# VectorE's low half of the next expert's second weights, moved behind the output operations in a mixture-of-experts loop

## Chip, cores and metric

One NeuronCore of a Trainium2 chip runs the program. The metric is the device time of one execution in microseconds, the median of several runs.

## The reference

The whole computation is one block of a graph network on 1250 nodes with 768 features: a layer norm, then a graph convolution over 20000 edges and a second-order linear attention over 12 heads, both added to the input, then a second layer norm and a switch layer of eight experts. Only the expert part is touched here:

```python
h = jax.nn.gelu(jnp.einsum('ecd,edf->ecf', buf[:E], w1) + b1[:, None, :], approximate=False)
o = jnp.einsum('ecf,efd->ecd', h, w2) + b2[:, None, :]
y_exp = o[routes, dest_c]
y = jnp.where(keep[:, None], y_exp, xf)
out = y * prob_max[:, None]
```

Each of the 8 experts has room for 195 rows (capacity), `w1` is 768 x 384 and `w2` 384 x 768 per expert. The result of each row, weighted by its gate, is added to the row before the switch layer.

## The kernel before

Everything runs in float32 accuracy, made of two reduced numbers: a matrix `A` is split into a high half `AH` (a rounded copy, made by ScalarE) and a low half `AL = A - AH` (made by VectorE), and each product is the three matmuls high x high, high x low and low x high (`product`, lines 2022 to 2030).

The expert loop is software-pipelined by hand over five engines, each with its own program and semaphores between them. Two experts are one turn of the `Fori` loop (`b` = 0, 1); the last pair is unrolled. For expert `e`:

- SyncE loads the weights into one staging buffer each, `w1s` and `w2s` (1152 KB each), and the second bias `b2r`. Its queue is in order: the bias of `e + 1` when the additions of `e - 1` are done (line 1776), the first weights of `e + 2` when VectorE has made `w1L` of `e + 1` (line 1780), the second weights of `e + 2` when it has made `w2L` of `e + 1` (line 1783).
- GpSimd issues the indirect transfers: it gathers the rows of `e + 2` (`xe`, line 1810), scatters the finished rows of `e` in two tiles of 105 and 90 rows (`out`, line 1839), and behind each scatter gathers the residual rows of `e + 1` (`x1g`, line 1818). When both scatters of `e` have landed (line 1845) it raises `oe_store` (line 1846), which lets VectorE write `oE` again.
- TensorE does the first product in three parts (line 2002), turns the rows of `e + 1` (line 1985), then does the second product in two tiles (line 2011). The second part of the first product waits until VectorE has read the second product of the expert before out of PSUM (`y_done`, line 2001).
- ScalarE makes `w1H` of `e + 1` (line 1857), the GELU and its high half `hH` (lines 1884, 1887), the high half of the turned rows (line 1869), and `w2H` of `e + 1` (line 1861).
- VectorE makes, in this order: `w1L` of `e + 1` (line 1903), the three parts of `hL` (line 1948), a small copy of the bias (line 1921), the three parts of `xeL` of `e + 1` (line 1927), a small copy of the gates (line 1932), `w2L` of `e + 1` (line 1907), and then for each of the two tiles an addition of the bias out of PSUM (line 1960, waits for the tile and for `oe_store`) and a scaling with the residual added (line 1965, waits for `x1g`). The four operations of lines 1960 and 1965 are the output operations.

`w2L` of `e + 1` is read by TensorE's second product of `e + 1`, one turn later, which waits for it at line 2008.

Of the kernel before, what the change touches and what calls it, by code (L numbers as in the profile page):

```python
# [89 lines left out]
def at(start, size):  # L90
    return bass.ds(start, size)
# [12 lines left out]
def build(nc, x, src, dst, gnn_w, gnn_b, w_qkv, b_qkv, w_proj, b_proj, sw, sb_, w1, b1, w2, b2, out,  # L104
          counts, keyd, vdram, odram, xfd, x1d, invd, lowd):
    ctx = ExitStack()
    with ctx:
# [14 lines left out]
        def right(stack, specs):  # L122
# [104 lines left out]
            ("PM", [T, N], F32), ("Ba", [T, NT, T], BF16), ("Bb", [T, N], BF16), ("same", [T, T], F32),  # L227
            ("place_i", [T, CAP], I32), ("place", [T, CAP], F32), ("far", [1, 2, E], F32)])
        _, csum, seatr, low, peak, heavy, mark, hid = region([
            ("before", [P, 4 * D + 6 * D], F32), ("csum", [T, 2, T], F32), ("seatr", [T, NT, HEAVY], F32R),  # L230
            ("low", [HEAVY, 2 * T], F32R), ("peak", [T, NT, NT], F32), ("heavy", [T, NT], F32),
# [71 lines left out]
        @block.sync  # L303
        def _(sp):
            for i in range(NT):
                move(sp, xn[:, i, :], x[i * T:(i + 1) * T, :], x_in[i // 2])
                if i == 1:
                    for wc in range(3):
                        sp.dma_start(w_staging(wc), w_parts[0][0][2 * wc * P:2 * (wc + 1) * P, :].rearrange(
                            "(k p) n -> p k n", p=P)).then_inc(w_early[wc], 16)  # L310
            sp.wait_ge(keys, 2)
            sp.dma_start(keyd[0:P, :], keyA[:]).then_inc(key_out, 16)
            sp.dma_start(keyd[P:, :], keyB[:]).then_inc(key_out, 16)
            for s_ in (1, 0):
                sp.dma_start(ws[:, s_], w_qkv[:, s_ * D:s_ * D + P].rearrange("(k p) n -> p k n", p=P)
                             ).then_inc(wqk_in[s_], 16)
            sp.wait_ge(key_out, 32)

            def load_keys(half, slot, c, n):

                sp.dma_start(kb[:, half, slot:slot + n, :], keyd[c:c + n, :].unsqueeze(0).broadcast_to([P, n, P])
                             ).then_inc(kb_in[half], 16)

            load_keys(0, 0, 0, EC)
            sp.wait_ge(w_lo, 3)
            load_keys(1, 0, EC, EC)
            for i in range(NT):
                sp.wait_ge(v_lo, 2 * i + 2)
                move(sp, vdram[:, i, :].rearrange("(j p) f -> p j f", p=T),
                     VS[:, i % 2].bitcast(F32).rearrange("p (j a) l f -> p j (a l f)", a=2), v_store[i % 2])  # L330
                if i == FIRST_EDGES + 1:
                    sp.wait_ge(idx_ready, 2)
                    load_keys(0, 0, 2 * EC, EC)
                if i == FIRST_EDGES + 3:
                    sp.wait_ge(idx_ready, 4)
                    load_keys(1, 0, 3 * EC, EARLY - 3 * EC)
                    load_keys(1, EARLY - 3 * EC, LONE, 1)
# [226 lines left out]
        def _(pe):  # L564
            pe.wait_ge(consts, 2)

            def turn_x(g):

                t0, nt = XGROUPS[g]
                pe.wait_ge(xn_done, t0 + nt)  # L570
                for u in range(FIRST_UNIT[g], FIRST_UNIT[g + 1]):
                    _, _, k0, nk = XUNITS[u]
                    if u >= 4:
                        pe.wait_ge(xt_lo, u - 3)
                    for k in range(nk):
                        for t in range(nt):
                            m = (k * nt + t) * T
                            ins = pe.transpose(ps[:, u % 4, m:m + T], xn[:, t0 + t, (k0 + k) * P:(k0 + k + 1) * P],
                                               ident[0:T, 0:T])
                    ins.then_inc(tr_done, 1)  # L580
# [1152 lines left out]
        def nodes_over(eng):  # L1733

            eng.wait_ge(agg_mm, NT)
            eng.wait_ge(pj_mm, NT)
            eng.wait_ge(lg_mm, NT)
            eng.wait_ge(ch_done, NT)
            eng.wait_ge(xf_done, NT)
            eng.wait_ge(lg_done, NT)  # L1740
            eng.wait_ge(x1_store[0], MOVED * NT // 2)
            eng.wait_ge(x1_store[1], MOVED * NT // 2)
# [153 lines left out]
        @block.vector  # L1896
        def _(dve):
            nodes_over(dve)
            order = Chain(dve, route_order, steps_before[0])

            def split_w1(e, b):
                dve.wait_ge(we_hi, 2 * e + 1)
                dve.tensor_tensor(w1L[:, b], w1s[:], w1H[:, b].bitcast(F32), ALU.subtract).then_inc(we_lo, 1)

            def split_w2(e, b):
                dve.wait_ge(we_hi, 2 * e + 2)
                dve.tensor_tensor(w2L[:, b], w2s[:], w2H[:, b].bitcast(F32), ALU.subtract).then_inc(we_lo, 1)

            split_w1(0, 0)
            dve.memset(x1g[:], 0.0)  # L1910
            dve.wait_ge(plain_store[0], MOVED * NT // 2)
            dve.wait_ge(plain_store[1], MOVED * NT // 2)
            dve.memset(xeH[:, :, CAP:].bitcast(F32), 0.0)
            dve.memset(xeL[:, :, CAP:].bitcast(F32), 0.0).then_inc(pads, 1)
            split_w2(0, 0)
            dve.wait_ge(b1_tr, 1)
            dve.tensor_copy(b1c[:].rearrange("p e m -> p (e m)"), ps[:, 3, 256:256 + E * FT]).then_inc(b1_done, 1)
            dve.wait_ge(b1_done, 1)

            def bias_of(e, b):  # L1920
                dve.tensor_scalar(b1cur[:, b, :], b1c[:, at(e, 1), :].rearrange("p o m -> p (o m)"), 1.0, None,
                                  ALU.mult).then_inc(b1cur_done, 1)

            def cut_rows(e):
                for n in range(3):
                    dve.wait_ge(xe_hi, 3 * e + (n + 1))
                    dve.tensor_tensor(xeL[:, 2 * n:2 * n + 2, 0:CAP],
                                      ps[:, n, 0:2 * CAPP].rearrange("p (k c) -> p k c", k=2)[:, :, 0:CAP],
                                      xeH[:, 2 * n:2 * n + 2, 0:CAP].bitcast(F32), ALU.subtract).then_inc(xe_lo, 1)

            def chance_of(e, b):
                dve.tensor_scalar(pcur[:, b, :], pmc[:, at(e, 1), :].rearrange("p o t -> p (o t)"), 1.0, None,
                                  ALU.mult)

            dve.sem_inc(y_done, FREE)
            dve.sem_inc(oe_done, FREE)
            bias_of(0, 0)
            chance_of(0, 0)
            cut_rows(0)

            def turn(m, last):
                for b in range(2):
                    e = 2 * m + b
                    if not (last and b == 1):
                        split_w1(e + 1, 1 - b)
                    for f in range(FT):
                        dve.wait_ge(hh_done, 3 * e + (f + 1))
                        dve.tensor_tensor(hL[:, f, :], h32[:, f, :], hH[:, f, :].bitcast(F32),
                                          ALU.subtract).then_inc(hl_done, 1)
                    if not (last and b == 1):  # L1950
                        bias_of(e + 1, 1 - b)
                        cut_rows(e + 1)
                        dve.wait_ge(oe_done, 2 * e + FREE)
                        chance_of(e + 1, 1 - b)
                        split_w2(e + 1, 1 - b)
                    dve.wait_ge(b2_in[b], m * 16 + 16)
                    for t, (r0, n) in enumerate(CTILES):
                        dve.wait_ge(m2_mm, 2 * e + (t + 1))
                        dve.wait_ge(oe_store, e + FREE)
                        dve.tensor_tensor(oE[0:n, t, :].rearrange("p (c d) -> p c d", c=2),  # L1960
                                          ps[0:n, 6 - 2 * t:8 - 2 * t, 0:HALF],
                                          b2r[0:n, b, :].rearrange("p (c d) -> p c d", c=2), ALU.add).then_inc(y_done, 1)
                        dve.wait_ge(y_done, 2 * e + (t + 1 + FREE))
                        dve.wait_ge(x1g_in[t], 16 * e + 16)
                        dve.scalar_tensor_tensor(out=oE[0:n, t, :], in0=oE[0:n, t, :], scalar=pcur[0:n, b, t:t + 1],
                                                 in1=x1g[0:n, t, :], op0=ALU.mult, op1=ALU.add).then_inc(oe_done, 1)

            with dve.Fori(0, LASTM) as m:
                turn(m, False)
            turn(LASTM, True)  # L1970
# [89 lines left out]
```

## Time and profile before

| what | value |
| --- | --- |
| median of three runs | 1019.64 us (1017.2 to 1021.0) |
| the profiled execution | 1020.73 us, of which the span of the core's instructions 1019.0 us |
| granted TensorE clock, mean | 0.948 of full speed |
| busy over the span | TensorE 89%, VectorE 75%, ScalarE 48%, GpSimd 35% |
| expert loop | from about 882 us to the end, some 135 us |
| chain that ended last, whole span | TensorE 55%, VectorE 18%, issue 11%, DMA 7% |

The busy shares are means over stages with different limits; the expert loop is the last eighth of the span. In the timelines below a row gives the start, the duration, the engine, the line of the kernel, the operation, what it writes and reads with shapes, how many such are merged in the row, and in brackets how long the engine was idle before it and what ended that.

### The profile page before, as it was taken

How to read it: one execution, taken by the hardware profiler on the slowest of the kernel's cores; microseconds unless marked ns; L12 is line 12 of the kernel's file. 1: busy time of each engine (PE TensorE's matmuls, PEld its weight loads, DVE VectorE, ACT ScalarE, POOL GpSimd, SP SyncE). 2: the span in 40 equal slices, each digit the busy share in tenths (PEclk: the TensorE clock that was granted, in tenths of full speed). 3: DMA queues.
4: the chain of work that ended last, by engine and by line, in shares of the span. 5: the costliest groups of instructions: out<-in, count | busy, mean ns of one | idle time of the engine just before them, and what ended most of it. 6: DMA issues, size and time to landing. Idle time of an engine off the chain costs nothing.

```text
span 1019.0 us, 15414 instructions
## 1 busy us (share of the span) xinstructions
PE 906.3 (89%) x5154; PEld 859.9 (84%) x5154; DVE 760.4 (75%) x1570; ACT 488.4 (48%) x720; POOL 359.7 (35%) x236
## 2 busy tenths in 40 slices
PE   2899789989989989999999899979999995499895
PEld 2899689989989989988988789969999995398884
DVE  6778459989989989989988798554666666567773
ACT  2221256766766766767667641340323222255540
POOL 1014455545445554654555620000000001526562
PEclk9899799999999999999999899998999995599998
DMA  9986462364464364355436379255676634767861
GB/s 275 353 146 176 93 123 32 65 114 81 63 114 81 60 113 78 59 110 83 66 44 146 57 118 207 60 147 129 186 204 183 168 122 132 213 200 239 273 203 47
DMA packets 137614, 136.70 MB, mean 134 GB/s; under 512 B 70561, under 2 KB 118276, under 8 KB 136545
## 3 DMA queue, kind: packets, MB, share of 16 engines
q1 hardware_dynamic: 109646, 119.29, 44.9%
q0 software_dynamic: 27520, 16.67, 11.7%
q8 instruction: 25, 0.41, 0.2%
q10 hardware_dynamic: 403, 0.17, 0.1%
q14 instruction: 20, 0.16, 0.1%
HBM read 94.31 MB, written 38.17 MB: 130 GB/s over the span
## 4 chain that ended last, share of the span: by engine, by line
PE 55%; DVE 18%; issue 11%; DMA 7%; ACT 5%; POOL 1%; SPq 1%; DVEq 0%; ACTq 0%; POOLq 0%
PE ps L2027 9%; PE ps L2028 9%; PE ps L2029 9%; PE ps L1202 7%; PE ps L1186 4%; PE ps L1187 4%; PE ps L1623 3%; DMA out<-oE,ids 3%; DVE Pl L1061 3%; PE ps L1624 3%; DVE Ph L1059 2%; ACT Ph L852 2%; DMA Cs<-counts 2%; PE ps L1162 1%; ACT Pf L874 1%
## 5 line engine op out<-in xcount | busy, mean ns | idle before, releaser
L388 POOL DMA_INDIRECT counts<-countc,idxu x157 | 274.3, 1747 | 258.6 <-DMA counts<-countc,idxu 222.5
L1061 DVE SCALAR_TENSOR_TENSOR Pl<-Pf,Ph 125x832 fp32r<-125x832 f32 (+1 forms) x180 | 184.2, 1027 | 44.0 <-ACT Ph L852 40.4
L874 ACT ACTIVATE Pf<-ps 125x832 f32<-125x832 f32 (+1 forms) x180 | 156.0, 867 | 127.2 <-PE ps L1187 119.1
L1202 PE MATMUL ps<-Ph,vsb 125*128 125x416 f32 (+1 forms) x360 | 133.4, 371 | 23.2 <-DVE Pl L1061 23.0
L1202 PE MATMUL ps<-Pl,vsb 125*128 125x416 f32 (+1 forms) x360 | 127.9, 355 | 0.0
L1202 PEld LDWEIGHTS ps<-Ph,vsb 125*128 125x128 f32 x360 | 68.6, 191 | 39.1 <-DVE Pl L1061 26.0
L2027 PE MATMUL ps<-wH,XH 128*125 128x384 f32 x240 | 84.5, 352 | 4.1 <-DVE wL L481 4.1
L2027 PE MATMUL ps<-XH,wqkH 128*128 128x416 f32 (+1 forms) x216 | 83.1, 385 | 4.4 <-DVE wqkL L299 2.4
L2028 PE MATMUL ps<-wL,XH 128*125 128x384 f32 x240 | 82.9, 346 | 0.0
L2029 PE MATMUL ps<-wH,XL 128*125 128x384 f32 x240 | 82.6, 344 | 0.0
L852 ACT ACTIVATE Ph<-Pf 125x832 fp32r<-125x832 f32 (+1 forms) x90 | 80.5, 895 | 0.8
L2029 PE MATMUL ps<-XH,wqkL 128*128 128x416 f32 (+1 forms) x216 | 77.4, 358 | 0.0
L2028 PE MATMUL ps<-XL,wqkH 128*128 128x416 f32 (+1 forms) x216 | 77.1, 357 | 0.0
L1623 PE MATMUL ps<-HH,CH 125*125 125x384 f32 (+1 forms) x200 | 69.0, 345 | 2.7 <-issue 1.8
L1202 PEld LDWEIGHTS ps<-Pl,vsb 125*128 125x128 f32 x360 | 69.0, 192 | 0.8
L1624 PE MATMUL ps<-HL,CH 125*125 125x384 f32 x200 | 68.5, 342 | 0.0
L1186 PE MATMUL ps<-MA,KHA 128*125 128x416 f32 (+1 forms) x180 | 66.3, 369 | 1.8 <-DVE MA L938 1.8
L1186 PE MATMUL ps<-MB,KHB 128*125 128x416 f32 (+1 forms) x180 | 65.5, 364 | 0.2 <-ACT Pf L874 0.2
L1187 PE MATMUL ps<-MB,KLB 128*125 128x416 f32 (+1 forms) x180 | 64.1, 356 | 0.0
L1187 PE MATMUL ps<-MA,KLA 128*125 128x416 f32 (+1 forms) x180 | 63.9, 355 | 0.0
L1059 DVE TENSOR_SCALAR Ph<-Pf 125x832 fp32r<-125x832 f32 (+1 forms) x90 | 55.1, 612 | 4.9 <-PE ps L1202 1.1
L1805 POOL MEMSET xe<- 105x1536 f32 x1 | 1.4, 1382 | 159.2 <-DVE lg L1450 159.2
(281 smaller groups left out, 2196.2 us busy)
## 6 DMA issues: line engine op xcount, KB each, us to landing
Cs<-counts SPq DMA_DIRECT2D x17, 546.9 KB
w1s<-L_ffn_w SPq DMA_DIRECT2D x8, 1152.0 KB, 6.4
w2s<-L_ffn_w SPq DMA_DIRECT2D x8, 1152.0 KB
odram<-OHL SPq DMA_DIRECT2D x12, 625.0 KB, 8.4
oS<-odram SPq DMA_DIRECT2D x10, 750.0 KB, 4.8
vdram<-VS SPq DMA_DIRECT2D x10, 672.0 KB
vsb<-vdram SPq DMA_DIRECT2D x12, 560.0 KB
kt<-keyd SPq DMA_DIRECT2D x5, 1280.0 KB
```

The costliest lines, as they stand in the source:

```text
L388: pool.indirect_dma_start(out=counts, out_offset=bass.IndirectOffsetOnAxis(ap=idxu[:, c:c + 1], axis=0), in_=countc[:, c:c + 1], in_offset ...
L852: act.activation(Ph[:, i % RING, :, 0:w], Pf[:, i % RING, :, 0:w], ACT.Identity, bias=1.0).then_inc(p_hiA, 1)
L874: act.activation(Pf[:, i % RING, :, 0:w], ps[0:T, 2 * (i % 2):2 * (i % 2) + 2, 0:w], ACT.Square, bias=1.0).then_inc(sq_done, 1)
L1061: dve.scalar_tensor_tensor(out=p, in0=f, scalar=1.0, in1=h.bitcast(F32), op0=ALU.add, op1=ALU.subtract).then_inc(p_lo, 1)
L1186: pe.matmul(out_, KH[a][:, kt * T:(kt + 1) * T], q, start=True, stop=False)
L1187: ins = pe.matmul(out_, KL[a][:, kt * T:(kt + 1) * T], q, start=False, stop=True)
L1202: ins = pe.matmul(ps[:, 4 + s % 2, 0:w], vsb[:, 2 * kp + t, a, :], part[:, m % RING, t, 0:w], start=(kp == 0 and t == 0 and part is Ph), s ...
L1623: pe.matmul(ps[0:T, b, 0:HALF], CH[0:k, i % 2, s_, :], HH[0:k, s_, cs], start=(s_ == 0), stop=False)
L1624: ins = pe.matmul(ps[0:T, b, 0:HALF], CH[0:T, i % 2, s_, :], HL[:, s_, cs], start=False, stop=(s_ == NT - 1))
L2027: pe.matmul(out, lh, rh, start=(k == 0), stop=False)
L2028: pe.matmul(out, lh, rl, start=False, stop=False)
L2029: ins = pe.matmul(out, ll, rh, start=False, stop=(k == tiles - 1))
```

## The change

In VectorE's program, `w2L` of the next expert is made behind the four output operations of the turn and not in front of them. It is still not made in the last turn. No other engine's program is changed, and no wait is added or removed.

```diff
                         cut_rows(e + 1)
                         dve.wait_ge(oe_done, 2 * e + FREE)
                         chance_of(e + 1, 1 - b)
-                        split_w2(e + 1, 1 - b)
                     dve.wait_ge(b2_in[b], m * 16 + 16)
                     for t, (r0, n) in enumerate(CTILES):
                         dve.wait_ge(m2_mm, 2 * e + (t + 1))
...
                         dve.scalar_tensor_tensor(out=oE[0:n, t, :], in0=oE[0:n, t, :], scalar=pcur[0:n, b, t:t + 1],
                                                  in1=x1g[0:n, t, :], op0=ALU.mult, op1=ALU.add).then_inc(oe_done, 1)
+                    if not (last and b == 1):
+                        split_w2(e + 1, 1 - b)
```

## Rows read from the trace of the kernel before

**Rows 1.** The chain that ended last, one turn of the loop: start us, us, what holds it.

```profile
948.62 0.52 issue
...
952.07 0.66 POOL out L1839
...
957.94 6.04 DMA out<-oE,ids
```

**Rows 2.** Timeline of VectorE, turns 3 and 4: start us, us, engine line operation output<-inputs.

```profile
948.64 0.96 DVE L1960 TENSOR_TENSOR oE<-ps,b2r 105x768 f32<-105x768 f32 x1 [1.51 <-POOLq L1846]
...
951.65 1.01 DVE L1965 SCALAR_TENSOR_TENSOR oE<-oE,pcur,x1g 90x768 f32<-90x768 f32 x1
952.59 2.55 DVE L1903 TENSOR_TENSOR w1L<-w1s,w1H 128x2304 fp32r<-128x2304 f32 x1
955.06 0.62 DVE L1948 TENSOR_TENSOR hL<-h,hH 128x196 fp32r<-128x196 f32 x2
956.84 0.36 DVE L1948 TENSOR_TENSOR hL<-h,hH 128x196 fp32r<-128x196 f32 x1 [1.15 <-ACT hH L1887]
...
960.01 2.56 DVE L1907 TENSOR_TENSOR w2L<-w2s,w2H 128x2304 fp32r<-128x2304 f32 x1 [1.10 <-ACT w2H L1861]
964.16 0.96 DVE L1960 TENSOR_TENSOR oE<-ps,b2r 105x768 f32<-105x768 f32 x1 [1.59 <-POOLq L1846]
```

**Rows 3.** Timeline of VectorE at the first and second output operations.

```profile
899.08 2.56 DVE L1907 TENSOR_TENSOR w2L<-w2s,w2H 128x2304 fp32r<-128x2304 f32 x1 [1.21 <-ACT w2H L1861]
901.56 0.95 DVE L1960 TENSOR_TENSOR oE<-ps,b2r 105x768 f32<-105x768 f32 x1
...
917.51 0.96 DVE L1960 TENSOR_TENSOR oE<-ps,b2r 105x768 f32<-105x768 f32 x1 [1.95 <-POOLq L1846]
```

**Rows 4.** Timeline of VectorE: output operations of experts 5 and 6.

```profile
979.31 0.96 DVE L1960 TENSOR_TENSOR oE<-ps,b2r 105x768 f32<-105x768 f32 x1 [1.23 <-POOLq L1846]
...
993.15 0.95 DVE L1960 TENSOR_TENSOR oE<-ps,b2r 105x768 f32<-105x768 f32 x1
```

**Rows 5.** Timeline of GpSimd: its calls for indirect transfers, with their time.

```profile
876.01 2.41 POOL L1810 DMA_INDIRECT xe<-xfd,ids  x1 [0.30 <-issue]
...
904.59 1.01 POOL L1839 DMA_INDIRECT out<-oE,ids  x1 [16.59 <-DVE oE L1965]
905.91 3.34 POOL L1818 DMA_INDIRECT x1g<-x1d,ids  x1 [0.30 <-DVE oE L1965]
...
920.94 3.94 POOL L1839 DMA_INDIRECT out<-oE,ids  x1 [0.30 <-issue]
...
952.07 4.21 POOL L1839 DMA_INDIRECT out<-oE,ids  x1 [0.30 <-issue]
...
957.94 0.98 POOL L1839 DMA_INDIRECT out<-oE,ids  x1 [0.30 <-issue]
```

**Rows 6.** Timeline of VectorE beside three of these calls.

```profile
874.95 2.54 DVE L1907 TENSOR_TENSOR w2L<-w2s,w2H 128x2304 fp32r<-128x2304 f32 x1
...
904.56 1.02 DVE L1965 SCALAR_TENSOR_TENSOR oE<-oE,pcur,x1g 90x768 f32<-90x768 f32 x1
905.51 2.54 DVE L1903 TENSOR_TENSOR w1L<-w1s,w1H 128x2304 fp32r<-128x2304 f32 x1
```

**Rows 7.** Timeline of all engines: TensorE's last matmul of expert 0's first output tile.

```profile
899.46 0.33 PE L2029 MATMUL ps<-w2H,hL 128*105 128x384 f32 x1
```

**Rows 8.** Timeline of SyncE's queue: issue of expert 7's first weights.

```profile
970.91 0.38 SPq L1749 DMA_DIRECT2D w1s<-L_ffn_w  x1
```

**Rows 9.** Timeline of ScalarE: copy of the first weights that follows the load.

```profile
962.90 2.13 ACT L1857 ACTIVATE w1H<-w1s 128x2304 fp32r<-128x2304 f32 x1 [2.93 <-DMA w1s<-L_ffn_w]
```

**Rows 10.** Busy time, clock and DMA by stretch, after that issue.

```profile
972.00:978.00 6.00, 5.97 (x39) 5.45 (x38) 4.56 (x7) 4.46 (x6) 3.04 (x3) 1.00 0.92 303
978.00:979.00 1.00, 1.00 (x7) 0.91 (x6) 0.08 (x1) 1.00 (x1) 0.00 (x0) 1.00 0.11 25
```

**Rows 11.** Timeline of GpSimd: second scatter of expert 5.

```profile
988.61 0.98 POOL L1839 DMA_INDIRECT out<-oE,ids  x1 [0.30 <-issue]
```

## The prediction

> **What bounds the kernel now.** The change lies in the last loop of the program, over eight experts, so I read that stretch alone: first the chain that ended last, then each engine's timeline against it. The page's chain is mostly TensorE over the whole span, but in the expert loop it is a ring between GpSimd, the DMA engines and VectorE. I call R the moment at which VectorE may begin the output operations of an expert (line 1960). In [rows 1] the chain goes from R = 948.62 through GpSimd's queue to the first scatter of `out` (952.07), through a call for `x1g` to the second scatter (957.94), and 6.04 us in that transfer's landing, until 963.98. [rows 2] show the next R just behind it, at 964.16: 15.52 us later, after VectorE had idled 1.59 us for GpSimd's release. From the second output (917.51, [rows 3]) to the sixth (979.31, [rows 4]) there are four such intervals, 61.80 us, mean 15.45. Neither VectorE nor TensorE has to be faster there. What has to be watched is what stretches GpSimd's calls and the second scatter's landing.
>
> **What GpSimd's calls cost.** The reader should compare calls of one kind in [rows 5]. A call takes 0.98 to 1.01 us when nothing is in its way (957.94, 904.59). The first scatter of a turn takes 4.21 us (952.07). It isn't the number of transfers outstanding: the call at 905.91 took 3.34 us with one recent scatter ahead of it, and the one at 957.94, with more behind it, took 0.98. What goes with the long ones is VectorE. In [rows 6] `w2L` itself runs 874.95 to 877.49, and the call that began inside it at 876.01 ended at 878.42, 0.93 us after it. The call at 905.91 began inside `w1L` (905.51 to 908.05) and ended at 909.25, 1.20 after it. The scatter at 952.07 ended at 956.28, 1.14 after `w1L` ended (952.59 + 2.55, [rows 2]). So a call that meets one of these long subtractions, with both inputs in SBUF, waits until it ends, and then does nearly all of its work, about 0.93 us. In the loop the wait seems to last to the end of the first `hL` behind `w1L` (955.06 + 0.35, then 0.87 to the end of the call). The cut of the next rows, whose source is in PSUM, lies just ahead of and beside the scatter at 957.94 without harm.
>
> **What moves.** One VectorE instruction per turn, `w2L` of the next expert, 2.55 us, seven of the eight of line 1907 (the first stands ahead of the loop). Nothing is added and no wait is new; the order of the increments of `we_lo` stays. Behind the outputs it stands at R + 3.95 (four output operations, 948.64 to 952.59, [rows 2]) and ends at R + 6.5; `w1L` of the turn after it, queued directly behind, runs to R + 9.0 instead of R + 6.5, and the `hL` behind that. I cost each consequence against R.
>
> *The place it leaves.* In steady turns `w2L` filled idle time of VectorE (ended 962.57, R at 964.16, [rows 2]): nothing gained there. Only where R isn't set by GpSimd is there a gain: for expert 0, where TensorE's first output tile was complete at 899.79 [rows 7] and VectorE came at 901.56, behind `w2L` [rows 3]: 1.7 us.
>
> *GpSimd.* The first scatter is issued at R + 3.4 (952.07 less 948.64), as now. It then meets `w2L` and `w1L` back to back. Consecutive VectorE instructions overlap slightly in the timeline (`w1L` starts at 952.59, the `hL` at 955.06, 2.47 us later), so I see no gap for GpSimd between them. The call therefore ends 2.47 us later, and 0.31 more if the third `hL`, whose input is ready by then, has to pass too (956.84 now, R + 8.2): 2.5 to 2.8 us. I take 2.6, as GpSimd seems to get in behind the first `hL`. Both later calls, and the second scatter, move by as much: **2.6 us per ring interval**.
>
> *TensorE.* Its second products need the `hL`, done at R + 8.6 now (956.84 + 0.36), at R + 9.9 then. Each output tile takes some 3.3 us (18 matmuls), so the first is done at about R + 13.5, well ahead of the next R at R + 18. Hidden; the cover is over 4 us. If it were gone, 1.3 us per turn would show.
>
> *SyncE and the loads.* SyncE's queue waits for `w2L` before it loads the next second weights, so that load, the `b2` load and the first-weights load behind it move too. Now the second weights are loaded ahead of R, from about R - 1.3. Then they start at about R + 6.8, `b2` behind them, and the first weights at R + 9.3 instead of R + 6.75 (970.91 less 964.16, [rows 8]). ScalarE's copies need them by R + 18 or later: with the present issue-to-landing of some 6 to 7.5 us (no more than 7.4 from issue to the copy at 962.90, [rows 9]) they are there by about R + 17. Its copy of 2.13 us then stands ahead of the next GELU at worst to R + 20; but VectorE doesn't come to the first `hL` of that turn before R' + 9.0, with R' at R + 18. Hidden, with some 5 us to spare.
>
> *The second scatter's landing.* This is the cost that no row of before has. After the first-weights load of [rows 8] the DMA engines move 303 GB/s at a 0.92 share for six us and are idle in the next [rows 10], and R comes at 979.31: the scatter lands when that backlog is through. Then the second weights and `b2` (1.18 + 0.32 MB) and the delayed first scatter (0.32 MB) come into the same stretch. Lower bound: nothing, if the scatter gets its share past the hardware queue, as all this starts before it. Upper bound: 3.6 MB from R + 8.2 at 330 GB/s (the six-us mean raised to a full share) ends at R + 19.1, with a last us until the landing is seen R + 20, against R + 18.1 by the calls alone: 2 us. A gain is excluded, since no load leaves this stretch. I take **0.9**, nearer the lower end, because the scatter's 0.28 MB already ran beside a full weight load in [rows 10] and shares rather than queues.
>
> **The sum**, against the profiled execution (1020.73 us, span 1019.0; the runs' median is 1019.64, 1.1 lower).
> - To the second output: the outputs of expert 0 start 1.7 earlier, but one of the three calls after the first scatter now meets `w2L` plus `w1L`. VectorE has done `w1L` at about 909.9 where it was 908.05; the blocked call ends at 911.2, and if it is the `x1g` call and not the second scatter, the latter ends at 912.5, against 910.52 now. With 0 to 1 us of DMA: +0.7 to +3.0, taken 1.5.
> - Four intervals: 4 x (2.6 + 0.9) = 14.0; ends 4 x 2.47 = 9.9 and 4 x (2.78 + 2) = 19.1.
> - From the sixth output to the seventh, 13.84 now (979.31 to 993.15, [rows 4]). No first weights are loaded there. The second scatter's call (988.61, [rows 11]) ends at R + 10.3, then at R + 12.9; as its landing takes at most 3.56 now (VectorE was held by `w2L` to the end), R comes at R + 15.4 to 16.6: +1.6 to +2.8, taken 2.1.
> - The end: outputs of expert 6 to the end of the span. `w2L` delays one call by a few us but that landing has slack; 0 to 1, taken 0.3.
>
> 1.5 + 14.0 + 2.1 + 0.3 = **17.9 us**, ends 12.2 and 25.9. 1020.73 + 17.9 is 1038.6; I say **1038.5**, that is 1.8% slower.
>
> **Rivals.**
> - *GpSimd isn't held by `w2L`* (not slower). If the long calls have another cause that stays where it is, say start-up of a burst, the ring keeps its 15.45 us, and the gains are 1.7 at the first output and up to 1.1 at the seventh: 1017.9; with 0 to 1 us of extra landing in four turns, up to 1022. It decides for no change as long as the first scatter's call stays near 4.2 us. For it: the scatter at 904.59 ran 1.01 us although a scaling with two SBUF inputs began at 904.56, so not every such operation holds a call [rows 5, 6]. Against it: the call at 876.01, which ended 0.93 after a `w2L`. 12%.
> - The Trainium skill, SBUF — State Buffer, "Who interferes with whom", speaks for this rival: `tensor_tensor` has no 2-port mode, takes only the read interface, and it infers that descriptor generation wants the write interface, so such an operation wouldn't stall a DMA issued from GpSimd. By that rule the time is the 1017.9 above. The trace disagrees so far (2.41 us for the call inside `w2L`, against 0.98), though an indirect call also reads its row numbers from SBUF, for which the same section would let the two contend. This is why I leave it a chance of its own.
> - *GpSimd gets in between `w2L` and `w1L`.* The call at 920.94 took 3.94 and not 4.21: it got in one boundary sooner than the others [rows 5]. Then the first scatter ends at R + 7.4, the `x1g` call meets `w1L` and ends at R + 10.2, and the second scatter is 1.2 late and not 2.6: 1.0 + 4 x (1.2 + 0.4) + 1.0 + 0.3 = 8.7, 1029.5. That boundary was used in one turn of the six. 12%.
> - *The transfers pile up more*, above 2 us an interval, or the longer waits of TensorE lower its clock (granted 1.00 in [rows 10]) and the second products come behind the ring: above 1047. 8%.
> - *Faster* by over 0.5%: only if moving the second weights away from R shortens the row gathers and these were in the ring, more than 1 us a turn; nothing in [rows 1] shows it. 3%.
>
> **Chances.** The forecast (12 to 26 us) 65%, the others as given. 0.5% is 5.1 us, about what a measurement of this kernel can tell from no change. Slower by more: 65 + 12 + 8 and a little of the first rival, 0.85; faster 0.03; within it 0.12. For 8 in 10 the range takes the forecast's case down to its end at 1032.9, reaches to the partial rival at 1029.5 less its spread, and up to 1046.5: 1028 to 1046.5.
>
> **What the profile after would show.** The first scatter's call (line 1839) at 6.7 to 7 us instead of 4.2 in five turns; `w2L` at R + 3.95; intervals of the `oE` additions of 18 to 20 us; the landing of the second scatter 6.0 to 8 us from its issue. VectorE's idle time before line 1960 grows from 1.6 to about 6 us. Calls that stay at 4.2 us with intervals of 15.5 would make the first part wrong, and calls of 6.8 with an unchanged landing the second.

## The result and the profile after

The changed kernel takes 1035.46 us (median of 4 runs, 1028.33 to 1037.37) against 1018.42 us (median of 4 runs of before): ratio 1.0151, 95% interval 1.0102 to 1.0201. It is slower, as forecast, and 3.0 us under the predicted 1038.5. The profiled execution of the changed kernel has a span of 1034.8 us, 15.8 more than before.

The page of the changed kernel, its span and the engines' busy shares:

```profile
span 1034.8 us, 15414 instructions
...
PE 904.8 (87%) x5154; PEld 859.4 (83%) x5154; DVE 759.6 (73%) x1570; ACT 488.3 (47%) x720; POOL 374.0 (36%) x236
```

The busy times are nearly those of before, except GpSimd's, 374.0 us against 359.7: 14.3 us more, in the same 236 instructions. The instructions didn't change; some of GpSimd's calls got longer. (VectorE's output operations are one line higher up in this kernel, 1959 and 1964.)

VectorE's timeline over one interval, R = 955.47 (columns as in [rows 2]):

```profile
955.47 0.96 DVE L1959 TENSOR_TENSOR oE<-ps,b2r 105x768 f32<-105x768 f32 x1 [7.24 <-POOLq L1846]
...
958.48 1.01 DVE L1964 SCALAR_TENSOR_TENSOR oE<-oE,pcur,x1g 90x768 f32<-90x768 f32 x1
959.41 2.55 DVE L1907 TENSOR_TENSOR w2L<-w2s,w2H 128x2304 fp32r<-128x2304 f32 x1
961.88 2.55 DVE L1903 TENSOR_TENSOR w1L<-w1s,w1H 128x2304 fp32r<-128x2304 f32 x1
964.35 0.62 DVE L1948 TENSOR_TENSOR hL<-h,hH 128x196 fp32r<-128x196 f32 x2
966.14 0.36 DVE L1948 TENSOR_TENSOR hL<-h,hH 128x196 fp32r<-128x196 f32 x1 [1.16 <-ACT hH L1887]
...
974.40 0.96 DVE L1959 TENSOR_TENSOR oE<-ps,b2r 105x768 f32<-105x768 f32 x1 [6.30 <-POOLq L1846]
```

`w2L` stands at R + 3.94, `w1L` directly behind it, and the next R comes 18.93 us later, after 6.30 us of idling for GpSimd's release; in [rows 2] that was 15.52 and 1.59. GpSimd in the same interval:

```profile
956.22 1.04 POOL L1810 DMA_INDIRECT xe<-xfd,ids  x1 [5.99 <-DMA out<-oE,ids]
...
958.89 6.41 POOL L1839 DMA_INDIRECT out<-oE,ids  x1 [0.30 <-issue]
965.60 1.05 POOL L1818 DMA_INDIRECT x1g<-x1d,ids  x1 [0.30 <-issue]
966.96 0.98 POOL L1839 DMA_INDIRECT out<-oE,ids  x1 [0.30 <-issue]
```

The first scatter's call takes 6.41 us where it took 4.21 [rows 5], and ends at 965.30, 0.87 after `w1L` (964.43). All calls behind it move by that much. The chain, SyncE's queue, and the DMA engines:

```profile
966.96 7.27 DMA out<-oE,ids
```

```profile
962.21 0.37 SPq L1753 DMA_DIRECT2D w2s<-L_ffn_w  x1
963.35 0.35 SPq L1757 DMA_DIRECT2D b2r<-L_ffn_b  x1
964.79 0.37 SPq L1749 DMA_DIRECT2D w1s<-L_ffn_w  x1
```

```profile
959.50:962.50 3.00, 3.00 (x16) 3.00 (x15) 3.00 (x2) 2.48 (x4) 3.00 (x1) 0.50 0.06 13
963.50:972.50 9.00, 8.65 (x61) 8.07 (x60) 3.44 (x9) 4.10 (x7) 4.86 (x4) 0.99 0.91 317
974.40:993.00 18.60, 15.83 (x94) 15.06 (x94) 11.33 (x15) 7.61 (x11) 11.73 (x6) 0.82 0.64 199
```

The landing of the second scatter takes 7.27 us from its issue (6.04 in [rows 1]). The second weights are now issued at R + 6.7 and the first at R + 9.3. The last fence has the granted clock, the DMA share and GB/s as its last three columns (its third row is the following interval, for later): from R + 4 to R + 7 the DMA engines do nearly nothing (0.06), since all that could feed them, the first scatter and both weight loads, waits for VectorE. Then they are nearly full (0.91) for nine microseconds. The same two stretches of the kernel before, at the same distance from its R of 948.64:

```profile
952.60:955.60 3.00, 3.00 (x29) 3.00 (x29) 3.00 (x4) 0.79 (x2) 3.00 (x1) 1.00 0.52 146
956.60:965.60 9.00, 8.65 (x59) 8.04 (x57) 5.94 (x9) 5.51 (x6) 3.73 (x4) 1.00 0.87 258
```

There the first stretch had a share of 0.52.

### The profile page after: what moved, and what is told of

It reads as the page before. It is cut to its first block, busy times and chain, and to the rows that moved or that the text cites. A ratio compares the mean times of both kernels' runs of the same rounds, so it can differ in the third digit from the quotient of the medians.

```text
span 1034.8 us, 15414 instructions
## 1 busy us (share of the span) xinstructions
PE 904.8 (87%) x5154; PEld 859.4 (83%) x5154; DVE 759.6 (73%) x1570; ACT 488.3 (47%) x720; POOL 374.0 (36%) x236
## 3 DMA queue, kind: packets, MB, share of 16 engines
q0 software_dynamic: 27520, 16.67, 11.5%
## 4 chain that ended last, share of the span: by engine, by line
DMA 45%; PE 23%; POOL 15%; issue 12%; DVE 2%; SPq 2%; ACT 1%; POOLq 0%; DVEq 0%
DMA counts<-countc,idxu 32%; POOL counts L388 13%; PE ps L2028 4%; PE ps L2029 4%; PE ps L2030 4%; DMA out<-oE,ids 4%; DMA counts<-zeros 3%; PE ps L1623 3%; PE ps L1624 3%; SPq L101 1%; DMA xn<-x 1%; PE ps L1654 1%; DMA counts<-ones 1%; DMA wst<-L_mix_w_proj 1%; DMA Cs<-counts 1%
```

## The experiments

Single executions differ by about a per cent here (those of the kernel before by 1011.66 to 1021.00 us), and the profiles differ by more than that ahead of the expert loop, in code that these kernels share but for some buffers: VectorE's memset of the padding of `xeL` (line 1914 of before) comes at 874.97 us in the profile of before and between 870 and 889 us in the others. So the experiments are compared by what lies behind that point: the loop's time (from this memset to the end of the span), and the mean of the four intervals from the second output addition to the sixth. For the kernel before these are 144.0 and 15.45 us, for the changed kernel 161.7 and 18.90. Both are of one profiled execution each. The last column has the execution time, a median where there were several; the kernel before, run again beside the experiments, had medians of 1017.74 to 1020.90.

| kernel | first scatter's call, us | second scatter issued, us after R | mean interval, us | loop, us | time, us (executions) |
| --- | --- | --- | --- | --- | --- |
| before | 3.94 to 4.22 | 9.0 to 9.3 | 15.45 | 144.0 | 1018.42 (4) |
| changed | 6.41 to 6.53 | 11.5 to 11.6 | 18.90 | 161.7 | 1035.46 (4) |
| loads late, one buffer | 1.5 to 4.3 | 8.0 to 9.3 | 18.88 | 166.6 | 1052.12 (1) |
| changed, second weights' load early | 6.40 to 6.53 | 11.5 to 11.6 | 18.30 | 158.8 | 1049.55 (1) |
| before, both loads together | 1.0 to 1.6 | 5.6 to 6.5 | 15.76 | 151.4 | 1026.94 (1) |
| changed, a third of `w2L` | 4.80 to 4.82 | 9.9 | 17.51 | 153.6 | 1036.01 (1) |
| changed, memset for `w2L` | 1.5 or 6.3 to 6.4 | 10.1 or 11.4 to 11.5 | 18.65 | 161.1 | 1037.33 (1) |
| changed, `w1L` behind `hL` | 3.93 to 4.06 | 9.0 to 9.2 | 17.65 | 155.4 | 1035.33 (1) |
| before, memset for `w1L` | 1.5 to 1.6 or 4.1 | 6.6 to 9.2 | 15.22 | 140.9 | 1020.82 (1) |
| before, `w1L` behind `hL` | 1.0 | 5.6 | 16.41 | 149.2 | 1021.32 (10) |
| before, row gathers behind the scatters | 1.0 | 7.7 to 8.0 | 23.82 | 196.2 | 1069.51 (6) |
| changed, row gathers behind the scatters | 1.0 | 11.2 to 11.3 | 29.14 | 223.8 | 1095.75 (1) |
| before, `w1L` in thirds | 1.0 to 1.6 | 5.6 to 6.8 | 14.88 | 140.2 | 1014.30 (10) |
| thirds, and `w2L` moved | 3.9 to 7.4 | 9.4 to 12.5 | 17.92 | 157.7 | 1030.84 (6) |

My theory was the prediction's: two terms, GpSimd's call held by VectorE's queue of long operations, and the moved loads beside the second scatter. The first two kernels were to take each term alone.

**Loads alone, first try.**

```diff
                         load_w1(e + 2)
-                        sp.wait_ge(we_lo, 2 * e + 4)
+                        sp.wait_ge(we_lo, 2 * e + 5)
                         sp.sem_inc(carrier, 1)
                         load_w2(e + 2)
```

> The kernel before, with one wait changed: SyncE loads the second weights of expert e + 2 once VectorE has made w1L of e + 2, at about R + 6.8, where the changed kernel loads them, and the b2 load and the next first weights follow it; VectorE's order is that of before. Theory (two terms: the calls held on GpSimd, 2.2 us an interval in the changed kernel, and the landing of the second scatter beside more loads, 1.3): the first scatter's call stays at 4.2 us, its second scatter still starts at R + 9.3, the landing goes from 6.0 to somewhere up to 7.3, intervals 15.5 to 16.8 us. Rival (the moved loads are the cause, and the long call only shows them): call 6.4, intervals 18.9 us.

The first scatter's calls took 1.5 to 4.3 us, no longer than before, as the theory has it, but the interval was 18.88, beyond its 16.8 and as long as the rival gives. Most of that is a wait that neither had. ScalarE's timeline in this kernel:

```profile
963.48 2.13 ACT L1861 ACTIVATE w2H<-w2s 128x2304 fp32r<-128x2304 f32 x1 [4.00 <-DMA w2s<-L_ffn_w]
```

In VectorE's old order `w2L` stands ahead of the outputs, and with the load this late it is itself late: ScalarE waited 4.00 us for the weights, VectorE behind it, and R (968.12) came behind `w2L`. So the interval doesn't price the landing. The chain shows the landing itself:

```profile
957.57 7.95 DMA out<-oE,ids
```

The second scatter was issued at R + 9.0 (R = 948.56) and took 7.95 us to land, until R + 17.0; the turns beside it took 7.42 and 7.95, against 5.7 to 6.5 in the kernel before. With the loads late and no longer call, the landing alone would have set an interval of about 17.1 us (an estimate: 9.0 + 7.95 and the some 0.17 from landing to R), 1.7 more than before. The experiment also shows that with the second weights loaded as late as in the changed kernel, the old order would have been no faster.

**Loads alone, second try.** With two staging buffers for the second weights (a second copy of `w2s`), the load can be issued a turn ahead, and nobody waits for it.

```diff
+                        load_w2(e + 2, b)
                         load_w1(e + 2)
-                        sp.wait_ge(we_lo, 2 * e + 4)
-                        sp.sem_inc(carrier, 1)
-                        load_w2(e + 2)
```

(Left out: the lines that give `w2s`, its load and its readers the second buffer.)

> VectorE's order of before, with two staging buffers for the second weights, so that their load can be issued a turn ahead, at about R + 6.8 just ahead of the first weights', without anyone waiting for it. This puts both weight loads beside the second scatter, as the changed kernel does, and nothing else. Theory: the first scatter's call 4.2 us, second scatter at R + 9.3, its landing up from 6.1 by 0.6 to 1.3 us, intervals 16.1 to 16.8. Rival (the loads don't reach the scatter, all is GpSimd's call): 15.45. Rival (the loads carry most of it): 17.5 or more.

The interval was 15.76, between two of the cases. But the calls weren't 4.2 us (1.0 to 1.6), and again another wait took over. The chain:

```profile
908.08 11.98 DMA w1s<-L_ffn_w
...
920.08 2.14 ACT w1H L1855
...
922.25 2.61 DVE w1L L1901
```

The first weights, queued behind the second, land after 11.98 us, and `w1L` comes late behind them; GpSimd's calls then pass ahead of it. The loop is 7.4 us longer. So the two loads together do cost, by delaying each other; what they cost the second scatter's landing this kernel can't tell.

**Calls alone.** The changed kernel with the same two buffers, and the load for `e + 2` issued when TensorE has the first output tile of `e`:

```diff
-                        sp.wait_ge(we_lo, 2 * e + 4)
+                        sp.wait_ge(m2_mm, 2 * e + 1)
                         sp.sem_inc(carrier, 1)
-                        load_w2(e + 2)
+                        load_w2(e + 2, b)
```

> The changed kernel with two staging buffers for the second weights, so that their load for e + 2 starts when TensorE has the first output tile of e, about where the kernel before loads them; VectorE's order is that of the changed kernel. Theory: the first scatter's call 6.4 us as in the changed kernel, second scatter at R + 11.5, landing near 6.0, intervals about 17.7. Rival (the loads are the cause): call 4.2, intervals 15.5.

```profile
973.57 6.40 POOL L1839 DMA_INDIRECT out<-oE,ids  x1 [0.30 <-issue]
...
981.64 0.96 POOL L1839 DMA_INDIRECT out<-oE,ids  x1 [0.30 <-issue]
```

Calls of 6.4 us, the second scatter at R + 11.5, intervals of 18.30. With the second weights' load out of the way 0.6 of the 3.45 us is gone and 2.85 stays. It was 0.6 more than the 17.7 expected: the landing (6.3 to 6.8 us from its issue) doesn't fall back to that of before (5.7 to 6.5). This kernel isn't quite "calls alone": the first weights' load still waits for the later `w1L` and goes out at R + 9.3, and the first scatter is late. How much of the 0.6 is due to which wasn't tested. Set beside the kernel with late loads, the two parts don't add up to the whole: late calls with one load early cost 2.85 us, late loads with calls as before 1.7 by the estimate above, and both together only 3.45. So the parts overlap, and there is no clean split between the call and the loads.

**The length of what stands there.** Low half for one third of the tile only, from expert 1 on:

```diff
-                        split_w2(e + 1, 1 - b)
+                        split_w2(e + 1, 1 - b, 1)
...
+                dve.tensor_tensor(w2L[:, b, 0:n], w2s[:, 0:n], w2H[:, b, 0:n].bitcast(F32), ALU.subtract).then_inc(we_lo, 1)
```

> The changed kernel with w2L made for one third of its columns only from expert 1 on (0.9 us in place of 2.55; the other two thirds of the low half are left at zero or as they were, so that part of the product is left out). Theory (the call is held until VectorE's queue of two-input operations ends): the first scatter's call gets shorter by the same 1.6 us, 6.4 to 4.8, and the interval goes from 18.9 to about 17.2. Rival (the order as such, not the length, costs the time): call 6.4, interval 18.9.

```profile
962.14 4.82 POOL L1839 DMA_INDIRECT out<-oE,ids  x1 [0.30 <-issue]
```

4.82 us, as expected to 0.02, and intervals of 17.51 (17.2 expected). The call follows the length of what VectorE has there one for one: 1.6 us less there, 1.6 less here, 1.4 in the interval (in which the loads, which wait for `w2L` and `w1L`, are earlier too).

**The kind of operation.** A memset of the same tile, which leaves the low half of the second weights out:

```diff
-                dve.tensor_tensor(w2L[:, b], w2s[:], w2H[:, b].bitcast(F32), ALU.subtract).then_inc(we_lo, 1)
+                dve.memset(w2L[:, b].bitcast(F32), 0.0).then_inc(we_lo, 1)
```

> The changed kernel with w2L set to zero by a memset of the same 128x2304 tile in the same place (about 2 us), which reads nothing; the low half of the second weights is left out of the product. Theory (only operations with two SBUF inputs hold a call): the first scatter's call gets its turn during the memset and takes 1.5 to 2 us; the second scatter, then at about R + 6.5, meets w1L and ends at about R + 9.7; intervals about 15.5 to 16. Rival (any VectorE operation on that place holds it): call about 5.9, interval about 18.3.

```profile
922.92 1.47 POOL L1839 DMA_INDIRECT out<-oE,ids  x1 [0.30 <-issue]
...
941.35 6.39 POOL L1839 DMA_INDIRECT out<-oE,ids  x1 [0.30 <-issue]
```

```profile
942.50 1.98 DVE L1907 MEMSET w2L<- 128x2304 f32 x1 [0.43 <-issue]
944.39 2.49 DVE L1903 TENSOR_TENSOR w1L<-w1s,w1H 128x2304 fp32r<-128x2304 f32 x1
```

Neither theory. In two of five turns the call took 1.5 us, in three 6.3 to 6.4, through the memset and `w1L`. The 0.43 us ahead of the memset needn't be free time: at least as much stands ahead of every memset of this tile, and another of 1536 elements (`x1g`, 1.34 us) has 0.27 there, which is about as much less as the memset is shorter. The profile can't tell whether VectorE was already at work in it. The same question with no `w1L` in the way: the kernel before with a memset in the place of `w1L` (that low half is left out).

```diff
-                        split_w1(e + 1, 1 - b)
+                        zero_w1(e + 1, 1 - b)
...
+                dve.memset(w1L[:, b].bitcast(F32), 0.0).then_inc(we_lo, 1)
```

> The kernel before with w1L of experts 1 to 7 set to zero by a memset of the same tile in the same place, directly behind the output operations, where w1L stands (that low half is left out of the product). No long two-input operation is then beside the first scatter's call. Theory (only operations with two SBUF inputs hold a call): the call takes 1.0 to 1.5 us in every turn. Rival (a memset holds it too, as some turns of the memset run suggest): in some turns at least 3.5 to 4 us, ending 0.9 us after the memset.

```profile
952.61 1.98 DVE L1907 MEMSET w1L<- 128x2304 f32 x1 [0.43 <-issue]
954.51 0.56 DVE L1952 TENSOR_TENSOR hL<-h,hH 128x196 fp32r<-128x196 f32 x2
```

```profile
953.36 2.37 POOL L1818 DMA_INDIRECT x1g<-x1d,ids  x1 [0.30 <-issue]
...
967.97 4.08 POOL L1839 DMA_INDIRECT out<-oE,ids  x1 [0.30 <-issue]
```

The call of 953.36 began inside the memset (to 954.59) and took 2.37 us where a free one takes 1.05; it ended 1.14 us after the memset, the same 1.14 as behind `w1L` in [rows 5]. The scatter at 967.97 took 4.08. So a long memset holds GpSimd's calls too, at times, and the rule that only two inputs in SBUF do is wrong. Other scatters get in ahead of it: the one at 951.58 took 1.48 us and ended 0.88 after the scaling before the memset (951.17 + 1.01). Why these and not the others, though each began 0.3 to 0.4 us into that scaling, stays open.

**Whether the sum of two operations is the cause.** `w1L` taken from the queue behind the outputs, in the changed kernel and in the kernel before:

```diff
-                    if not (last and b == 1):
-                        split_w1(e + 1, 1 - b)
                     for f in range(FT):
...
                     if not (last and b == 1):
+                        split_w1(e + 1, 1 - b)
                         bias_of(e + 1, 1 - b)
```

> The changed kernel with w1L of the next expert made behind the three hL instead of in front of them: the first scatter's call then meets w2L alone. Theory (a call is held for as long as VectorE's long subtractions are queued back to back): the call returns to about 4.1 us, second scatter at R + 9.3, intervals 15.5 to 16.8. Rival (w2L's new place costs its time through something else than the call, such as the loads): 18 or more.

> The kernel before, w2L in its old place, and w1L of the next expert made behind the three hL and not behind the output operations. No long operation is then queued behind the outputs. Theory (the ring is set by held calls plus the landing): first scatter's call 1.5 us, second scatter at R + 6.6, landing by R + 13; VectorE then has 2.55 us more between hL and the next outputs (hL done at R + 8.6, w1L to 11.1, cuts to 12.6, w2L to 15.1) and becomes the bound at about 15.1: intervals 15.1, time 0 to 3 us under before. Rival (bytes in flight set the landing, wherever the scatter is issued): intervals 15.5 to 16.5.

In the first the call returned to 3.93 to 4.06 us, but the intervals only to 17.65, above the range given. In two of the four, `w1L` in its later place held the second scatter (2.83 us). In the other two it held only the `x1g` call behind it (3.26), the second scatter went out at R + 9.0 as before, and the intervals were still 17.06 and 16.71: the landing took 7.86 and 7.52 us. So here too 1.3 to 1.6 us are lost in the transfers with no call longer than before; of the loads, the second weights' now goes out at R + 6.7 and the first at R + 13.0. In the second kernel neither a scatter nor an `x1g` call was held (row gathers took up to 3.5 us), the second scatter was issued at R + 5.6, and yet the interval was 16.41, not 15.1 (ratio to before 1.0036, 1.0003 to 1.0068). That number lies in the rival's range. ScalarE's timeline there:

```profile
951.00 2.13 ACT L1857 ACTIVATE w1H<-w1s 128x2304 fp32r<-128x2304 f32 x1 [6.92 <-DMA w1s<-L_ffn_w]
```

`w1L` at R + 9 lets SyncE load the next first weights only then, and ScalarE waits 6.92 us for them, with the GELU queued behind. Free calls are worth nothing where a load takes their place as the last to arrive.

**GpSimd's row gathers behind its scatters**, on both kernels:

```diff
             for e in range(E):
-                if e + 2 < E:
-                    pool.wait_ge(xe_tr, 3 * e + 3)
-                    fetch_rows(e + 2)
                 for t, (r0, n) in enumerate(CTILES):
...
                         fetch(e + 1, t)
+                if e + 2 < E:
+                    pool.wait_ge(xe_tr, 3 * e + 3)
+                    fetch_rows(e + 2)
```

> The kernel before with GpSimd's two row gathers of expert e + 2 issued behind the two scatters and the x1g gathers of e instead of in front of them, 2.7 us less ahead of the first scatter. Theory (the ring through GpSimd sets the interval): the first scatter starts at R + 2.9 and takes 1.0 us, the x1g call behind it is held by w1L to about R + 7.6, the second scatter starts at R + 7.9 instead of R + 9.3; intervals 14.1 to 14.9 instead of 15.45, the kernel 4 to 8 us faster than before. Rival (the landing is set by the bytes in flight, not by when the scatter is issued): intervals stay at 15.4 and the time is that of before.

> The same reordering of GpSimd's gathers, on the changed kernel. Theory: first scatter's call 1.0 us, the x1g call held by w2L and w1L to about R + 9.9, second scatter at R + 10.2 instead of R + 11.5, intervals 17.6 instead of 18.9. Rival (the landing is set by the bytes in flight): 18.9.

Both expectations failed: 1.0462 (1.0407 to 1.0518) on the kernel before, intervals of 23.8, and 29.1 on the changed one. The second scatter was issued at R + 7.8 as expected (11.2 on the changed kernel, where 10.2 was expected), but the chain doesn't go through it:

```profile
936.80 5.00 DMA xe<-xfd,ids
...
941.85 2.21 PE ps L1985 x12
```

TensorE turns these rows in the same interval, and now waits for them. I had taken them for an expert further ahead. The pair still says something: the same move of `w2L` costs 5.3 us an interval here, where `x1g`, second scatter and row gathers all queue behind the held call. That call, for the first `x1g`, takes 6.5 to 6.6 us instead of 3.1 to 3.4; what the other 2 us are wasn't taken apart.

**A kernel without the held call, and the change on top of it.** `w1L` in thirds, one behind each `hL`, in the time in which VectorE waits for the GELU:

```diff
                     for f in range(FT):
                         dve.wait_ge(hh_done, 3 * e + (f + 1))
                         dve.tensor_tensor(hL[:, f, :], h32[:, f, :], hH[:, f, :].bitcast(F32),
                                           ALU.subtract).then_inc(hl_done, 1)
+                        if not (last and b == 1):
+                            part_w1(e + 1, 1 - b, f)
```

> The kernel before with w1L made in three parts of 0.9 us, one behind each hL, in VectorE's waits for the GELU. Theory (a call waits only for what is queued back to back): the first scatter's call 1.5 to 2.7 us, second scatter at R + 8.0 to 8.5 instead of R + 9.3, VectorE free in time for R + 14; intervals about 14.5, time 4 to 7 us under before. Rival (the landing is set by the bytes in flight): intervals stay at 15.4.

Calls of 1.0 to 1.6 us, intervals of 14.88, loop 3.8 us shorter than before. Over ten runs the median is 1014.30 and the ratio to before 0.9962 (0.9916 to 1.0008), not clear of no change. It is the only kernel here with an interval and a median under those of before that computes all. On it, the studied change:

```diff
                         chance_of(e + 1, 1 - b)
-                        split_w2(e + 1, 1 - b)
...
                                                  in1=x1g[0:n, t, :], op0=ALU.mult, op1=ALU.add).then_inc(oe_done, 1)
+                    if not (last and b == 1):
+                        split_w2(e + 1, 1 - b)
```

> The studied change applied to the kernel with w1L in thirds behind the hL: w2L goes from in front of the output operations to behind them, so that the first scatter's call meets w2L and no whole w1L. Without the move the calls of that kernel take 1.0 to 1.6 us, its second scatter starts at R + 5.6 in most turns, and its intervals average 14.9. Theory (the place directly behind the outputs is what costs, whatever is put there): first scatter's call 3.9 to 4.2 us, second scatter at R + 9, intervals 16 to 17.6, the kernel 5 to 18 us above before. Rival (the change costs only because w1L already stood there and the two add up): intervals under 15.5, the time that of before or less.

The ratio to before is 1.0127 (1.0082 to 1.0172), intervals of 17.92 against 14.88: the move costs 3.0 us an interval here too, with no whole `w1L` behind it. The interval lies above the 16 to 17.6 expected. The forecast of 4 us for the call held in one turn of five; in the others it took 5.1 or 7.4. VectorE and GpSimd from R = 931.75:

```profile
935.70 2.54 DVE L1914 TENSOR_TENSOR w2L<-w2s,w2H 128x2304 fp32r<-128x2304 f32 x1
938.16 0.35 DVE L1953 TENSOR_TENSOR hL<-h,hH 128x196 fp32r<-128x196 f32 x1
938.44 0.95 DVE L1908 TENSOR_TENSOR w1L<-w1s,w1H 128x768 fp32r<-128x768 f32 x1
939.30 0.35 DVE L1953 TENSOR_TENSOR hL<-h,hH 128x196 fp32r<-128x196 f32 x1
939.58 0.94 DVE L1908 TENSOR_TENSOR w1L<-w1s,w1H 128x768 fp32r<-128x768 f32 x1
940.45 0.35 DVE L1953 TENSOR_TENSOR hL<-h,hH 128x196 fp32r<-128x196 f32 x1
940.72 0.95 DVE L1908 TENSOR_TENSOR w1L<-w1s,w1H 128x768 fp32r<-128x768 f32 x1
```

```profile
918.32 3.94 POOL L1839 DMA_INDIRECT out<-oE,ids  x1 [0.31 <-issue]
...
935.18 7.38 POOL L1839 DMA_INDIRECT out<-oE,ids  x1 [0.31 <-issue]
```

Seven operations without a gap, from 935.70 to 941.67, and the call ends at 942.56, 0.89 behind the last. In the turn at 918.32, where VectorE idled 0.45 us behind `w2L`, it took 3.94. So a call can be held by more than one instruction, and the short `hL` between two longer operations didn't let it in here. But it isn't simply VectorE's unbroken queue either. Behind the last third here the bias copy and the `xeL` follow at once, and in the changed kernel:

```profile
996.40 6.41 POOL L1839 DMA_INDIRECT out<-oE,ids  x1 [0.31 <-issue]
```

```profile
999.39 2.55 DVE L1903 TENSOR_TENSOR w1L<-w1s,w1H 128x2304 fp32r<-128x2304 f32 x1
1001.86 0.90 DVE L1948 TENSOR_TENSOR hL<-h,hH 128x196 fp32r<-128x196 f32 x3
1002.68 0.16 DVE L1921 TENSOR_SCALAR b1cur<-b1c 128x3 f32<-128x3 f32 x1
1002.75 1.49 DVE L1927 TENSOR_TENSOR xeL<-ps,xeH 128x390 fp32r<-128x390 f32 x3
```

This call ended at 1002.81, 0.87 behind `w1L`, though VectorE went on without a gap to 1004.3. The held scatters looked at here end some 0.9 us behind an operation of 0.94 us or longer, or one `hL` later (1.14). Why a boundary in front of a short operation serves at one place and not at another isn't shown.

## Why the prediction was right

*The terms.* The profiled spans allow the sum to be taken apart as it was made.

| term | predicted | measured |
| --- | --- | --- |
| start of the loop to the second output | +1.5 | 917.36 - 917.51, less the -1.87 by which the memset of `xeL` is earlier (873.10 against 874.97): +1.72 |
| four intervals | +14.0 | 75.61 - 61.80 = +13.81 |
| sixth to seventh output | +2.1 | 16.13 - 13.84 = +2.29 |
| the end | +0.3 | 25.70 - 25.85 = -0.15 |
| ahead of the loop | 0 | -1.87 |
| sum | +17.9 | +15.8 |

The loop costs 17.7 us. The 2.1 us between forecast and measurement are mostly the part ahead of the loop, which the change doesn't touch and which varies from one execution to the next.

*Within the four intervals* the two parts were off in opposite ways, so that the total, 13.8 for 14.0, is closer than its terms, and that is luck. The call was priced at 2.6 and is 2.2 longer (6.4 to 6.5 us, just under the 6.7 to 7 given as the sign): I reckoned with GpSimd getting in behind the first `hL`, as before, and in this kernel it gets in right behind `w1L` (0.87 us after it, in five turns of five). What I put down to the landing was priced at 0.9 and is 3.45 - 2.2 = 1.25; the bounds of 0 and 2 held. Taking the second weights' load away gave 0.6 of it back. The rest is spread over the first weights' load, `b2` and the late first scatter, which no run takes apart. And the sum of a call and a landing is itself rougher than it looks: late loads without a longer call cost 1.3 to 1.7 us an interval.

*The first output* came earlier, at 897.54 or 24.44 us behind the memset of `xeL` where it was 26.59, so 2.15 earlier and not 1.7; and the `x1g` call was the one held (902.25, 6.22 us), the worse of the two cases given. Hence 1.72 and not less.

*The covers* held, but more thinly than I had worked out. The `hL` were done at R + 11.0 (966.14 + 0.36) and not at R + 9.9. TensorE had sat idle 3.21 us for the output additions, from about R - 0.2, and was then granted 0.50, the lower of its two levels (1.2 GHz), from about R + 1.4 to R + 8.3. Its first output tile was complete at 970.02 (R + 14.6, not R + 13.5). In the interval from 974.40 its mean clock was 0.82, and the profile puts the end of VectorE's idle time before the next output (992.97) down to TensorE. That is a misreading to avoid: TensorE's last product for the first tile is

```profile
989.42 0.33 PE L2030 MATMUL ps<-w2H,hL 128*105 128x384 f32 x1
```

and was done 3.2 us before that output, which came 0.17 us behind the second scatter's landing (986.03 + 6.77), just as in the turns put down to GpSimd; the matmul named is the last of the second tile. So GpSimd's release set R here too, and a cover of over 4 us had shrunk to 3.2. The rival of the clock (part of the 8%) cost nothing over the ring. The first weights landed after 10.5 us instead of 7.2, at R + 19.8 and not R + 17, and the slack took that as well.

*The rival of no held call*, 12%, fell with the first scatter's 6.4 us. The Trainium skill (SBUF — State Buffer, "Who interferes with whom") infers that `tensor_tensor` doesn't keep GpSimd from writing descriptors; for indirect calls this case's trace goes the other way, 6.41 us against 0.98, and the third of `w2L` shows it one for one. It agrees with what the same section says of an instruction with two SBUF inputs beside a GpSimd instruction that reads SBUF, if the reading of the row numbers counts as that. The section also says that an instruction with at most one SBUF input outside the two-port modes doesn't contend; the call of 2.37 us beside a memset speaks against it, unless the memset ran in such a mode, which no run here shows. What the wait is made of no run here shows.

*The rival of getting in between* `w2L` and `w1L`, 12%, never came up: no call of the changed kernel ended there.

*Where a step was weak:* the explanation of which operations hold a call (two inputs in SBUF) was argued from rows in which nothing else was long, and the memset runs refute it. The price didn't depend on it, since `w2L` itself was seen holding a call. That nothing in the chain made the row gathers matter was true only because they were in time: the gathers put behind the scatters cost 4.6%.

## What to carry to other kernels

Filler work of one engine isn't free where it is put just because that engine is idle later: ask which other engine's issue it holds, and put long operations where that engine has nothing to issue. Here one 2.55 us instruction moved past four others left every engine's busy time but GpSimd's alone and cost 3.5 us a turn, because it lengthened the run of operations behind which the next scatter is issued, and put off two loads. When an operation gates a load, its place is also the load's place; price the transfers that follow it, and look at the stretches in which the DMA engines now have nothing.

## What the runs showed of the hardware that I had not expected

- A GpSimd indirect call held behind VectorE mostly ends 0.87 to 0.93 us behind the last long operation of a run: 7.38 us in all behind seven back-to-back operations, 3.94 where a 0.45 us gap came sooner. Short operations that follow the last long one without a gap mostly didn't hold it further.
- A memset of 128x2304 float32, 1.98 us, reads nothing and held calls at times, one for 2.37 us where a free one takes 1.05. At the start of such a memset some calls got in (1.48 us) and some were held through it (6.39, 4.08).
- The profile's releaser can be the wrong one: 5.13 us of VectorE's idle time are put down to a matmul whose tile it wasn't waiting for.
- Two weight loads of 1152 KB queued one behind the other let the second land after 10.1 to 12.0 us; in the kernel before, with the two apart, the first weights took a median of 7.2.
